# One operand format changed: the FFN's matmuls of a scan-and-FFN kernel take fp32 operands instead of two fp16 parts of each

## The chip, the cores and the metric

The kernel runs on 1 core of one Trainium2 chip. The metric is the device time of one execution in microseconds (us). Before the change it was 1563.5 us, the median of 3 runs (1563.49 to 1563.74).

## What is computed

The reference, cut to what matters (B = 8 rows, T = 256 time steps, N = 512 neurons, I = 1408 hidden units):

```python
# L0_cond: 256 steps of RK4 over q, p [8, 512]; drive is x, coupling [512, 512]
i_couple = tanh(q) @ coupling.T
dq = q - q**3 / 3 - p + drive + i_couple + bias      # four times in each step
dp = EPSILON * (q + ALPHA - BETA * p)
q, p = clip(rk4(q, p))                               # every q is kept: [8, 256, 512]
# L0_ffn on the 2048 rows of the q that were kept
w_gu = dequant_fp4(gate_up_packed, gate_up_scales)   # [2816, 512]
w_down = dequant_fp4(down_packed, down_scales)       # [512, 1408]
gate, up = split(q_trace @ w_gu.T)
y = (silu(gate) * up) @ w_down.T
out = x + y / sqrt(mean(y * y) + 1e-6)
```

The scan is serial: each of its 256 x 4 evaluations needs the one before. The FFN of a row needs only that row.

## The kernel before, in words

**Setup.** The weights arrive packed, in 11 units (`UNITS`). A unit holds, for 128 hidden features, the four 128-column tiles of the gate weights, the four of the up weights and the 512 columns of the down weights: 1536 columns (`UW`). For each unit SyncE issues two DMAs (`raw`, `sc`; three buffers, so that unit u + 3 is issued when `dq_w32` says that unit u is unpacked), VectorE runs three instructions (L547, L550, and L555, which writes fp32 `w32`), ScalarE rounds `w32` to the fp16 high part `wffn[:, u, 0]` (L513), and GpSimd forms the fp16 low part `wffn[:, u, 1]` by a subtraction (L501). Between units 3 and 4 VectorE also makes the scan's weights (L566). All engines meet at the end of the setup before the scan begins.

**Scan.** The program is 16 blocks (`BLOCKS`) of 16 time steps; a block has 64 stages (4 evaluations a step). In a stage TensorE multiplies `tanh(q)` (fp16 high and low part, `th`) by `wscan` in 32 small matmuls (L607), VectorE reduces the result into the next `q` in two halves (L722, L724), ScalarE takes the next tanh (L643, L645), and TensorE begins the next stage. While TensorE works, VectorE forms the low part of tanh (L683) and the terms of q alone (L677 to L695).

**FFN.** It lies one block behind the scan. After its 32 scan matmuls, and before those of the next stage, TensorE issues in program order the FFN matmuls that a table (`plan.pe`) gives to this stage. `hist` keeps the q of a block (128 tokens). In stages 0 to 2 of the next block ScalarE and VectorE turn it into two fp16 parts, `xh` (L393) and `xl` (L398). Each gate or up weight tile then takes four fp16 matmuls of 128 columns (high and low weight by `xh` and `xl`, L346): 32 for each unit. ScalarE applies silu (L370), VectorE multiplies (`h32`, L377), ScalarE and VectorE split `h32` into `hh` and `hl` (L384, L389), and eight fp16 matmuls of 256 columns (L360) add the unit to `y_ps`. A unit's down matmuls come at least `DOWN_LAG` = 7 stages after its gate and up matmuls. At the end of an FFN block the sum of squares, its root and the output rows follow.

`ffn_schedule` charges a gate or up matmul 1 and a down matmul 2 and gives every stage the same budget of 8; the last unit's eight down matmuls come late and fall into stage 6 of the block after. `Places` hands out the stages in which VectorE gets `h32` and `hl`. The first FFN block has a table of its own (`FIRST_SCHEDULE`), which starts at stage 6 with 13 or 14 matmuls a stage.

Of the kernel before, what the change touches and what calls it, by code (L numbers as in the profile page):

```python
# [120 lines left out]
GU_PARTS = 4  # L121
DOWN_PARTS = 4
DOWN_LAG = 7
START_LATE = 4
CATCH_UP = 6


def ffn_schedule(late, catch_up):


    gate_ups = [(u, j) for u in range(UNITS) for j in range(2 * GU_PARTS * KT)]
    downs = [(u, j) for u in range(UNITS) for j in range(2 * DOWN_PARTS)]
    down_cost = N // 2 // P
    even = (len(gate_ups) + down_cost * (len(downs) - 2 * DOWN_PARTS)) / STAGES
    at, done, budget, s = {}, {}, 0.0, FFN_FIRST
    while gate_ups or downs:
        if s >= FFN_FIRST + late + catch_up:
            budget += even
        elif s >= FFN_FIRST + late:
            budget += even * (late + catch_up) / catch_up  # L140
        while gate_ups or downs:
            down_now = downs and s >= done.get(downs[0][0], s) + DOWN_LAG
            if not (down_now or gate_ups) or budget < (down_cost if down_now else 1):
                break
            u, j = (downs if down_now else gate_ups).pop(0)
            at.setdefault(s, []).append(("down" if down_now else "gate_up", u, j))
            budget -= down_cost if down_now else 1
            if not down_now and j == 2 * GU_PARTS * KT - 1:
                done[u] = s
        s += 1  # L150
    return at, done


class Places:


    def __init__(self):
        self.taken = {1, 2}

    def next(self, s):  # L160
        while s % 4 not in (1, 2) or s % STAGES in self.taken:
            s += 1
        self.taken.add(s % STAGES)
        return s


class Schedule:


    def __init__(self, late, catch_up):  # L170
        self.pe, gate_up = ffn_schedule(late, catch_up)
        places = Places()
        self.silu = {s + 1: u for u, s in gate_up.items()}
        self.h32, self.hh, self.hl = {}, {}, {}
        for u, s in gate_up.items():
            at = places.next(s + 2)
            self.h32[at] = self.hh[at] = u
            self.hl[places.next(at + 1)] = u
# [7 lines left out]
    def rest(self):  # L186

        return [{s: x for s, x in part.items() if s >= STAGES} for part in
                (self.pe, self.silu, self.h32, self.hh, self.hl)] + [self.norm_sum]


SCHEDULE = Schedule(0, 0)
FIRST_SCHEDULE = Schedule(START_LATE, CATCH_UP)
assert FIRST_SCHEDULE.rest() == SCHEDULE.rest()
# [3 lines left out]
class Signals:  # L198


    def __init__(self, new, tag, parity):
# [19 lines left out]
        self.xh_ready = sem("xh_ready")  # L221
        self.xl_ready = sem("xl_ready")
# [3 lines left out]
        self.hh_ready = sem("hh_ready")  # L226
        self.hl_ready = sem("hl_ready")
# [10 lines left out]
def program(nc, x, drive, cond_t, coupling_t, bias_t, packed, scales, out):  # L238
# [8 lines left out]
    with ctx:  # L247
# [4 lines left out]
        hist = sb("hist", [P, KT, STEPS, B])  # L252
# [18 lines left out]
        wffn = sb("wffn", [P, UNITS, 2, UW], F16)  # L271
# [49 lines left out]
        dq_hi = sem("dq_hi")  # L321
        dq_lo = sem("dq_lo")
# [12 lines left out]
        def gate_up(pe, f, g, u, j):  # L335

            b = (u + f.parity) % 2
            half, r = divmod(j, GU_PARTS * KT)
            kt, which = divmod(r, GU_PARTS)
            part, tokens = ((0, xh), (0, xl), (1, xh), (1, xl))[which]  # L340
            col = (half * KT + kt) * P
# [6 lines left out]
            if j == 2 * GU_PARTS * KT - 1:  # L348
                i.then_inc(f.gu_ready, 1)

        def down(pe, f, u, j):

            b = (u + f.parity) % 2
            if j == 0:
                pe.wait_ge(f.hl_ready, u + 1)
            which, half = divmod(j, 2)
            part, h = ((0, hh), (0, hl), (1, hh), (1, hl))[which]
            cols = slice(half * N // 2, (half + 1) * N // 2)

            i = nc.tensor.matmul(y_ps[f.parity][:, cols], h[b][:, :], wffn[:, u, part, 2 * KT * P:][:, cols],  # L360
                                 start=(u == 0 and j == 0), stop=(u == UNITS - 1 and which == DOWN_PARTS - 1),
                                 skip_group_check=True)
            if j == 2 * DOWN_PARTS - 1:
                i.then_inc(f.down_done, 1)

        def ffn_silu(act, f, g, u):
# [4 lines left out]
                                 scale=1.0 / W_SCALE).then_inc(f.silu_ready, 1)  # L371

        def ffn_h32(dve, f, g, u):
            b = (u + f.parity) % 2
            dve.wait_ge(f.silu_ready, u + 1)
            wait_unit(dve, lambda s: s.hl_ready, f, g, u)
            nc.vector.scalar_tensor_tensor(h32[b][:, :], gu_ps[b][:, P:2 * P], H_SCALE / W_SCALE,  # L377
                                           silu[b][:, :], ALU.mult, ALU.mult).then_inc(f.h32_ready, 1)

        def ffn_hh(act, f, g, u):  # L380
            b = (u + f.parity) % 2
            act.wait_ge(f.h32_ready, u + 1)
            wait_unit(act, lambda s: s.down_done, f, g, u)
            nc.scalar.activation(hh[b][:, :], h32[b][:, :], ACT.Copy).then_inc(f.hh_ready, 1)  # L384

        def ffn_hl(dve, f, u):
            b = (u + f.parity) % 2
            dve.wait_ge(f.hh_ready, u + 1)
            nc.vector.tensor_tensor(hl[b][:, :], h32[b][:, :], hh[b][:, :], ALU.subtract).then_inc(f.hl_ready, 1)  # L389

        def hist_high(act, f, c):

            nc.scalar.activation(xh[f.parity][:, c, :], hist[:, c].rearrange("p t b -> p (t b)"), ACT.Copy,  # L393
                                 scale=1.0 / S).then_inc(f.xh_ready, 1)
# [27 lines left out]
        def act_ffn(act, plan, f, g, s):  # L422
# [3 lines left out]
            if s in plan.hh:  # L426
                ffn_hh(act, f, g, plan.hh[s])
# [3 lines left out]
        def dve_ffn(dve, plan, f, g, s):  # L431
# [3 lines left out]
            if s in plan.hl:  # L435
                ffn_hl(dve, f, plan.hl[s])
# [35 lines left out]
        with nc.Block() as block:  # L472
# [23 lines left out]
            def _(pool):  # L496
                nc.gpsimd.iota(shift[:, :], [[0, 1]], base=P - 1, channel_multiplier=-1).then_inc(iota_done, 1)
                nc.gpsimd.memset(mhalf[:, :], -0.5)
                for u in range(UNITS):
                    pool.wait_ge(dq_hi, u + 1)  # L500
                    nc.gpsimd.tensor_tensor(wffn[:, u, 1, :], w32[u % UNPACK_BUFS][:, :], wffn[:, u, 0, :],  # L501
                                            ALU.subtract).then_inc(dq_lo, 1)

            @block.scalar
            def _(act):
# [5 lines left out]
                for u in range(UNITS):  # L511
                    act.wait_ge(dq_w32, u + 1)
                    nc.scalar.activation(wffn[:, u, 0, :], w32[u % UNPACK_BUFS][:, :], ACT.Copy).then_inc(dq_hi, 1)  # L513
                    if u == 1:
                        act.wait_ge(coup_in, 16)
                        for n, coef in enumerate(COEF):
                            nc.scalar.activation(wscan[:, n, 0], coup[:, :, :], ACT.Copy,
                                                 scale=coef * S).then_inc(coup_hi, 1)

            @block.vector  # L520
            def _(dve):
# [9 lines left out]
                nc.vector.tensor_scalar(hist[:, :, STEPS - 1, :], q_raw[:, :, :], S, None, ALU.mult)  # L531
# [8 lines left out]
                link(nc.vector.tensor_copy(q_raw[:, :, :], hist[:, :, STEPS - 1, :]))  # L540

                def unpack(u):
# [10 lines left out]
                    if u >= UNPACK_BUFS:  # L553
                        dve.wait_ge(dq_lo, u - UNPACK_BUFS + 1)
# [394 lines left out]
```

## Time and profile before

| | |
|---|---|
| median of 3 runs | 1563.5 us |
| the profiled execution, its time | 1563.14 us |
| its span | 1561.4 us |
| TensorE busy (matmul) | 1434.9 us, 92% |
| TensorE weight load busy | 1306.2 us, 84% |
| VectorE busy | 1486.6 us, 95% |
| ScalarE busy | 785.3 us, 50% |
| GpSimd busy | 48.4 us, 3% |

The span is the profiled execution from its first to its last instruction; 1.7 us lie around it. The durations of matmuls are latencies: consecutive ones overlap, so a stream's pace is read from the distance between starts, or from a merged piece divided by its count. "Idle before" is the time in which the engine stood still ahead of an instruction, and the name behind the arrow is what ended it.

### The profile page before, as it was taken

To read this page: it belongs to the slowest core of one execution; us is meant where nothing else is said; L and a number is where in the kernel's file an instruction comes from. 1 tells how busy PE (TensorE), PEld (TensorE's weight loads), DVE (VectorE), ACT (ScalarE), POOL (GpSimd) and SP (SyncE) were. 2 spreads that over 40 slices of the span, in tenths; PEclk is the share of its full clock that TensorE was granted. 3 is DMA by queue.
4 is the path that set the end of the run, shared out by engine and by line. 5 is a ranking of instruction groups with operands and counts; after the bars stand their busy time and mean duration, and the time that the engine had idled before them with its cause. 6 is when DMAs were issued, how large, how long until landed. Compare 5 with 4: busy or idle time off the path is not lost.

```text
span 1561.4 us, 96622 instructions
## 1 busy us (share of the span) xinstructions
PE 1434.9 (92%) x39808; PEld 1306.2 (84%) x39808; DVE 1486.6 (95%) x11021; ACT 785.3 (50%) x5087; POOL 48.4 (3%) x49
## 2 busy tenths in 40 slices
PE   0047799999999999999999999999999999999997
PEld 0046799999999899999999999999989999999997
DVE  7989999999999999999999999999999999999992
ACT  4134455555555555555555555555555555555552
POOL 3410000000000000000000000000000000000000
PEclk9999999999999999999999999999999999999999
DMA  9500000000000000000000000000000000000000
GB/s 236 131 6 7 14 8 7 5 21 8 21 8 21 8 4 22 7 21 7 21 8 11 18 5 21 8 21 8 21 8 4 21 8 21 8 21 7 10 15 22
DMA packets 13548, 33.08 MB, mean 21 GB/s; under 512 B 1712, under 2 KB 6064, under 8 KB 12976
## 3 DMA queue, kind: packets, MB, share of 16 engines
q1 hardware_dynamic: 13104, 26.89, 6.6%
q8 instruction: 311, 5.10, 1.4%
q14 instruction: 133, 1.09, 0.2%
HBM read 22.69 MB, written 4.19 MB: 17 GB/s over the span
## 4 chain that ended last, share of the span: by engine, by line
DVE 82%; PE 10%; issue 2%; ACT 0%; DVEq 0%; POOLq 0%; POOL 0%; ACTq 0%
DVE th L683 12%; DVE with_q L677 9%; DVE scan_ps L695 8%; DVE q_cub L690 7%; DVE q_sq L687 7%; DVE q_stage L724 7%; DVE p_part L677 6%; DVE q_stage L722 6%; PE scan_ps L607 5%; PE gu_ps L346 4%; DVE with_p L677 3%; DVE q_raw L724 3%; DVE hist L706 3%; DVE h L377 3%; DVE q_raw L722 2%; DVE hl L389 2%
## 5 line engine op out<-in xcount | busy, mean ns | idle before, releaser
L607 PE MATMUL scan_ps<-th,wscan 128*128 128x32 f16 (+1 forms) x32768 | 1045.0, 175 | 118.0 <-ACT th L643 115.6
L607 PEld LDWEIGHTS scan_ps<-th,wscan 128*128 128x128 f16 x32768 | 939.2, 96 | 235.6 <-ACT th L643 179.6
L643 ACT ACTIVATE th<-q_stage 128x16 f16<-128x16 f32 x1536 | 318.4, 207 | 493.6 <-DVE q_stage L722 493.6
L346 PE MATMUL gu_ps<-xl,wffn 128*128 128x128 f16 x2816 | 385.2, 219 | 0.0
L346 PE MATMUL gu_ps<-xh,wffn 128*128 128x128 f16 x2816 | 384.7, 218 | 0.0
L683 DVE TENSOR_TENSOR th<-t,th 128x16 f16<-128x16 f32 x2048 | 351.5, 172 | 5.4 <-ACT t L645 5.4
L645 ACT ACTIVATE t<-q_stage 128x16 f32<-128x16 f32 x1536 | 306.1, 199 | 0.0
L346 PEld LDWEIGHTS gu_ps<-xl,wffn 128*128 128x128 f16 x2816 | 273.0, 97 | 0.3
L346 PEld LDWEIGHTS gu_ps<-xh,wffn 128*128 128x128 f16 x2816 | 262.9, 97 | 0.3
L643 ACT ACTIVATE th<-q_raw 128x16 f16<-128x16 f32 x512 | 106.2, 207 | 188.3 <-DVE q_raw L722 184.8
L452 ACT ACTIVATE sum_r<-dr,constant 128x64 f32<-128x64 f32 x528 | 174.1, 332 | 8.0 <-DMA dr<-drive 8.0
L724 DVE TENSOR_REDUCE q_stage<-scan_ps 128x16 f32<-128x48 f32 x768 | 159.7, 208 | 0.3
L722 DVE TENSOR_REDUCE q_stage<-scan_ps 128x16 f32<-128x48 f32 x768 | 157.5, 205 | 1.2 <-PE scan_ps L607 1.2
L695 DVE SCALAR_TENSOR_TENSOR scan_ps<-with_q,q_cub 128x32 f32<-128x32 f32 x768 | 152.2, 198 | 0.0
L687 DVE SCALAR_TENSOR_TENSOR q_sq<-q_stage 128x32 f32<-128x32 f32 x768 | 143.8, 187 | 3.4
L690 DVE SCALAR_TENSOR_TENSOR q_cub<-q_sq,q_stage 128x32 f32<-128x32 f32 x768 | 144.9, 189 | 0.0
L677 DVE SCALAR_TENSOR_TENSOR p_part<-p_part,q_stage 128x32 f32<-128x32 f32 x768 | 143.4, 187 | 0.0
L677 DVE SCALAR_TENSOR_TENSOR with_q<-hist,with_p 128x32 f32<-128x32 f32 x768 | 141.6, 184 | 0.0
L677 DVE SCALAR_TENSOR_TENSOR with_q<-q_stage,with_q 128x32 f32<-128x32 f32 x768 | 141.3, 184 | 0.0
L360 PE MATMUL y_ps<-wffn,hh 128*128 128x256 f16 x704 | 133.7, 271 | 2.3 <-DVE hl L389 2.3
L360 PE MATMUL y_ps<-wffn,hl 128*128 128x256 f16 x704 | 134.1, 272 | 0.0
L645 ACT ACTIVATE t<-q_raw 128x16 f32<-128x16 f32 x512 | 102.0, 199 | 0.0
(43 smaller groups left out, 990.8 us busy)
## 6 DMA issues: line engine op xcount, KB each, us to landing
raw<-packed SPq DMA_DIRECT2D x11, 768.0 KB, 6.2
dr<-drive SPq DMA_DIRECT2D x34, 128.0 KB, 3.3
sc<-scales SPq DMA_DIRECT2D x11, 384.0 KB, 6.3
xres<-x SPq DMA_DIRECT2D x16, 256.0 KB, 3.6
out<-osb SPq DMA_DIRECT2D x16, 256.0 KB, 2.9
coup<-coupling_t SPq DMA_DIRECT2D x1, 1024.0 KB, 15.7
q_raw<-cond_t SPq DMA_DIRECT2D x1, 16.0 KB, 1.8
bias<-bias_t SPq DMA_DIRECT2D x1, 2.0 KB, 1.7
```

What stands on the lines that cost most here:

```text
L346: i = nc.tensor.matmul(gu_ps[b][:, half * P:(half + 1) * P], wffn[:, u, part, col:col + P], tokens[f.parity][:, kt, :], start=(r == 0), st ...
L360: i = nc.tensor.matmul(y_ps[f.parity][:, cols], h[b][:, :], wffn[:, u, part, 2 * KT * P:][:, cols], start=(u == 0 and j == 0), stop=(u == ...
L607: i = nc.tensor.matmul(to if both else to[:, 0], wscan[:, w, part, kt, cols], moving if both else moving[:, 0], start=first, stop=last, sk ...
L643: nc.scalar.activation(th[s % 2][:, c, 0, :], q[:, c, :], ACT.Tanh, scale=1.0 / S).then_inc(now.tanh_hi, 1)
L645: nc.scalar.activation(t32[:, c, :], q[:, c, :], ACT.Tanh, scale=1.0 / S).then_inc(now.tanh_32, 1)
L677: return local(nc.vector.scalar_tensor_tensor(to, x, factor, base, ALU.mult, ALU.add))
L683: nc.vector.tensor_tensor(th[s % 2][:, c, 1, :], t32[:, c, :], th[s % 2][:, c, 0, :], ALU.subtract).then_inc(now.tanh_lo, 1)
L687: return local(nc.vector.scalar_tensor_tensor(q_sq[:, :, :], q, CUBE[i], q, ALU.mult, ALU.mult))
L690: return local(nc.vector.scalar_tensor_tensor(q_cub[:, :, :], q_sq[:, :, :], OWN[i], q, ALU.add, ALU.mult))
L695: nc.vector.scalar_tensor_tensor(local_ps, halves(linear[i]), UNIT[i], halves(q_cub[:, :, :]), ALU.mult, ALU.add).then_inc(now.first_half, 1)
L722: nc.vector.tensor_reduce(q_next[:, 0:HC, :], three[0], AX.X, ALU.add).then_inc(now.q_ready, 1)
L724: nc.vector.tensor_reduce(q_next[:, HC:KT, :], three[1], AX.X, ALU.add).then_inc(now.q_ready, 1)
```

## The change

`xh`, `xl`, `hh`, `hl`, `w32` and all that makes them are gone. VectorE's third unpacking instruction writes `wffn` in fp32 directly. The gate and up matmuls read `hist` in fp32 (now two buffers, one for each parity of blocks, since TensorE reads it during the whole block), and the down matmuls read `h32` in fp32. So a gate or up weight tile takes one matmul instruction where it took four, and a unit's down weights take two of 256 columns where they took eight. In one FFN block there are 88 gate and up matmuls and 22 down matmuls. They are dealt out by their number alone: gate and up number n goes to stage 2 + n * 64 // 88, down number n to a first stage + n * 64 // 22. The first FFN block uses the same table. `Places` now lets VectorE's `h32` fall into every stage that is not the fourth of its step.

```diff
-GU_PARTS = 4
-DOWN_PARTS = 4
-DOWN_LAG = 7
-START_LATE = 4
-CATCH_UP = 6
...
+DOWN_PARTS = 2
...
-    def __init__(self, late, catch_up):
-        self.pe, gate_up = ffn_schedule(late, catch_up)
+    def __init__(self):
+        gate_ups = [(u, j) for u in range(UNITS) for j in range(2 * KT)]
+        downs = [(u, j) for u in range(UNITS) for j in range(DOWN_PARTS)]
+        gate_up_at = [FFN_FIRST + n * STAGES // len(gate_ups) for n in range(len(gate_ups))]
+        done = [gate_up_at[(u + 1) * 2 * KT - 1] for u in range(UNITS)]
...
+        down_first = max(s - DOWN_PARTS * u * STAGES // len(downs) for u, s in enumerate(ready))
+        self.pe = {}
+        for n, (u, j) in enumerate(downs):
+            self.pe.setdefault(down_first + n * STAGES // len(downs), []).append(("down", u, j))
+        for n, (u, j) in enumerate(gate_ups):
+            self.pe.setdefault(gate_up_at[n], []).append(("gate_up", u, j))
...
-        hist = sb("hist", [P, KT, STEPS, B])
+        hist = [sb(f"hist{i}", [P, KT, STEPS, B]) for i in range(2)]
...
-        wffn = sb("wffn", [P, UNITS, 2, UW], F16)
+        wffn = sb("wffn", [P, UNITS, UW])
...
-            if u == 0 and half == 0 and which == 0:
-                pe.wait_ge(f.xl_ready, kt + 1)
-            i = nc.tensor.matmul(gu_ps[b][:, half * P:(half + 1) * P], wffn[:, u, part, col:col + P],
-                                 tokens[f.parity][:, kt, :], start=(r == 0), stop=(r == GU_PARTS * KT - 1))
...
+            i = nc.tensor.matmul(gu_ps[b][:, half * P:(half + 1) * P], wffn[:, u, j * P:(j + 1) * P],
+                                 hist[1 - f.parity][:, kt].rearrange("p t b -> p (t b)"),
+                                 start=(kt == 0), stop=(kt == KT - 1))
...
-                pe.wait_ge(f.hl_ready, u + 1)
...
+                pe.wait_ge(f.h32_ready, u + 1)
+            cols = slice(j * N // DOWN_PARTS, (j + 1) * N // DOWN_PARTS)
+            i = nc.tensor.matmul(y_ps[f.parity][:, cols], h32[b][:, :], wffn[:, u, 2 * KT * P:][:, cols],
+                                 start=(u == 0 and j == 0), stop=(u == UNITS - 1), skip_group_check=True)
...
-        def ffn_hh(act, f, g, u):
...
-        def ffn_hl(dve, f, u):
...
-        def hist_high(act, f, c):
...
-        def hist_low(dve, f, c):
...
-                for u in range(UNITS):
-                    pool.wait_ge(dq_hi, u + 1)
-                    nc.gpsimd.tensor_tensor(wffn[:, u, 1, :], w32[u % UNPACK_BUFS][:, :], wffn[:, u, 0, :],
-                                            ALU.subtract).then_inc(dq_lo, 1)
...
-                for u in range(UNITS):
-                    act.wait_ge(dq_w32, u + 1)
-                    nc.scalar.activation(wffn[:, u, 0, :], w32[u % UNPACK_BUFS][:, :], ACT.Copy).then_inc(dq_hi, 1)
...
-                    if u >= UNPACK_BUFS:
-                        dve.wait_ge(dq_lo, u - UNPACK_BUFS + 1)
-                    nc.vector.scalar_tensor_tensor(w32[b][:, :], fp4, FP4_BITS * W_SCALE, sc[b][:, :],
+                    nc.vector.scalar_tensor_tensor(wffn[:, u, :], fp4, FP4_BITS, sc[b][:, :],
                                                    ALU.mult, ALU.mult).then_inc(dq_w32, 1)
...
-                if ffn and t == 1:
-                    dve.wait_ge(now.xl_ready, KT)
+                ffn_part(s)
+                if t == 1 and rest:
+                    dve.wait_ge(before.gu_ready, UNITS)
```

**TensorE, in the steady part of a block.** Before, a stage with four down matmuls is followed by the 32 scan matmuls (12 with one tanh part, 20 with two) and by a stage with eight gate matmuls:

```order
L360 MATMUL y_ps<-wffn,hh 128x256 x2
L360 MATMUL y_ps<-wffn,hl 128x256 x2
L607 MATMUL scan_ps<-th,wscan 128x2x8 x12
L607 MATMUL scan_ps<-th,wscan 128x2x2x8 x20
L346 MATMUL gu_ps<-xh,wffn 128x128
L346 MATMUL gu_ps<-xl,wffn 128x128
L346 MATMUL gu_ps<-xh,wffn 128x128
L346 MATMUL gu_ps<-xl,wffn 128x128
L346 MATMUL gu_ps<-xh,wffn 128x128
L346 MATMUL gu_ps<-xl,wffn 128x128
L346 MATMUL gu_ps<-xh,wffn 128x128
L346 MATMUL gu_ps<-xl,wffn 128x128
```

Now, in a steady block too, a stage with one down and one gate matmul, then one with two gate matmuls, then one with one:

```order
L318 MATMUL y_ps<-wffn,h_1 128x256
L306 MATMUL gu_ps<-hist,wffn 128x128
L529 MATMUL scan_ps<-th,wscan 128x2x8 x12
L529 MATMUL scan_ps<-th,wscan 128x2x2x8 x20
L306 MATMUL gu_ps<-hist,wffn 128x128 x2
L529 MATMUL scan_ps<-th,wscan 128x2x8 x12
L529 MATMUL scan_ps<-th,wscan 128x2x2x8 x20
L306 MATMUL gu_ps<-hist,wffn 128x128
L529 MATMUL scan_ps<-th,wscan 128x2x8 x12
L529 MATMUL scan_ps<-th,wscan 128x2x2x8 x20
```

Four fp16 matmuls have become one fp32 matmul, and a stage now has one, two or three of them. Counted in fp16 matmuls of 128 columns (a down matmul of 256 columns is two), every stage had 8; if an fp32 matmul stands for four, a stage now has 4, 8, 12 or 16. Over the 64 stages of a block whose table overlaps the end of the one before, 24 stages have one gate matmul, 18 have two, 16 have one gate and one down, and 6 have two gates and one down.

**TensorE, stage 6 of a block.** Before, the last unit's eight down matmuls of the block before meet eight gate matmuls:

```order
L360 MATMUL y_ps<-wffn,hh 128x256 x2
L360 MATMUL y_ps<-wffn,hl 128x256 x2
L360 MATMUL y_ps<-wffn,hh 128x256 x2
L360 MATMUL y_ps<-wffn,hl 128x256 x2
L346 MATMUL gu_ps<-xh,wffn 128x128
L346 MATMUL gu_ps<-xl,wffn 128x128
L346 MATMUL gu_ps<-xh,wffn 128x128
L346 MATMUL gu_ps<-xl,wffn 128x128
L346 MATMUL gu_ps<-xh,wffn 128x128
L346 MATMUL gu_ps<-xl,wffn 128x128
L346 MATMUL gu_ps<-xh,wffn 128x128
L346 MATMUL gu_ps<-xl,wffn 128x128
```

This pile of 24 (in the same count) is gone: the last unit's two down matmuls fall into stages 5 and 8, one in each, with one gate matmul beside each.

**ScalarE, the setup.** Before, eleven roundings of whole units stand between the drive sums and the scan:

```order
L452 ACTIVATE sum_r<-dr,constant 128x8x8 x16
L513 ACTIVATE wffn<-w_0 128x1536
L513 ACTIVATE wffn<-w_1 128x1536
L517 ACTIVATE wscan<-coup 128x2048 x3
L513 ACTIVATE wffn<-w_2 128x1536
L513 ACTIVATE wffn<-w_0 128x1536
```

Now:

```order
L384 ACTIVATE sum_r<-dr,constant 128x8x8 x16
L441 ACTIVATE wscan<-coup 128x2048 x3
L404 UNCONDITIONAL_BRANCH
L800 UNCONDITIONAL_BRANCH
L567 ACTIVATE th<-q_raw 128x2x8
```

The roundings are gone, and with them GpSimd's eleven subtractions; VectorE's three instructions a unit stand in the same order as before.

## Rows read from the trace of the kernel before

**Rows 1.** The page, its first line.

```profile
span 1561.4 us, 96622 instructions
```

**Rows 2.** Busy time by stretch; (x) is instructions, then PEclk, DMA share, GB/s.

```profile
25.00:30.00 5.00, 0.00 (x0) 0.00 (x0) 4.93 (x4) 4.64 (x3) 1.51 (x2) 1.00 1.02 246
...
90.00:120.00 30.00, 21.26 (x649) 19.17 (x650) 27.28 (x207) 13.58 (x94) 1.42 (x1) 1.00 0.03 8
...
800.00:900.00 100.00, 99.88 (x2787) 90.60 (x2784) 98.23 (x771) 53.40 (x357) 0.74 (x2) 1.00 0.05 14
```

**Rows 3.** Timeline of VectorE: first reductions of chosen stages.

```profile
181.73 0.21 DVE L722 TENSOR_REDUCE q_stage<-scan_ps 128x16 f32<-128x48 f32 x1
...
197.74 0.21 DVE L722 TENSOR_REDUCE q_stage<-scan_ps 128x16 f32<-128x48 f32 x1
...
199.27 0.21 DVE L722 TENSOR_REDUCE q_raw<-scan_ps 128x16 f32<-128x48 f32 x1
...
272.61 0.21 DVE L722 TENSOR_REDUCE q_stage<-scan_ps 128x16 f32<-128x48 f32 x1
...
817.48 0.20 DVE L722 TENSOR_REDUCE q_stage<-scan_ps 128x16 f32<-128x48 f32 x1
...
819.58 0.21 DVE L722 TENSOR_REDUCE q_raw<-scan_ps 128x16 f32<-128x48 f32 x1 [0.69 <-PE scan_ps L607]
...
830.55 0.21 DVE L722 TENSOR_REDUCE q_raw<-scan_ps 128x16 f32<-128x48 f32 x1
...
1433.66 0.21 DVE L722 TENSOR_REDUCE q_stage<-scan_ps 128x16 f32<-128x48 f32 x1
```

**Rows 4.** The chain in order of time, the last 40 us: start, us, what.

```profile
1522.05 0.32 ACT xh L393
...
1522.40 0.90 DVE xl L398 x4
...
1525.27 4.47 PE gu_ps L346 x80
...
1529.73 0.87 PE y_ps L360 x8
...
1553.45 0.32 ACT hh L384
...
1553.79 0.30 DVE hl L389
```

**Rows 5.** Timeline of the setup: start, us, engine, line.

```profile
44.04 1.01 DVE L547 TENSOR_SCALAR nib<-raw,shift 128x1536 int32<-128x1536 int32 x1
...
47.76 1.01 DVE L547 TENSOR_SCALAR nib<-raw,shift 128x1536 int32<-128x1536 int32 x1
...
54.24 1.01 DVE L547 TENSOR_SCALAR nib<-raw,shift 128x1536 int32<-128x1536 int32 x1
...
88.33 3.09 POOL L501 TENSOR_TENSOR wffn<-w,wffn 128x1536 f16<-128x1536 f32 x1 [3.21 <-ACT wffn L513]
...
91.75 0.21 ACT L643 ACTIVATE th<-q_raw 128x16 f16<-128x16 f32 x1 [3.49 <-PEq L472]
```

**Rows 6.** Groups of the setup on VectorE: xcount, busy us, mean ns.

```profile
L555 DVE SCALAR_TENSOR_TENSOR w<-nib,sc 128x1536 f32<-128x1536 f16 x11 | 41.6, 3778 | 0.4
...
L550 DVE TENSOR_SCALAR nib<-nib 128x1536 int32<-128x1536 int32 x11 | 13.3, 1211 | 0.4
...
L566 DVE SCALAR_TENSOR_TENSOR wscan<-coup,wscan 128x2048 f16<-128x2048 f32 x3 | 9.6, 3241 | 0.0
```

**Rows 7.** DMA issues of the setup: KB each, median us to landing.

```profile
sc<-scales SPq DMA_DIRECT2D x11, 384.0 KB, 6.3
```

**Rows 8.** Groups of FFN instructions on TensorE: busy us, mean ns.

```profile
L346 PEld LDWEIGHTS gu_ps<-xl,wffn 128*128 128x128 f16 x2816 | 273.0, 97 | 0.3
```

**Rows 9.** Timeline of TensorE in the first FFN block.

```profile
190.74 0.31 PE L346 MATMUL gu_ps<-xh,wffn 128*128 128x128 f16 x1
...
190.84 0.31 PE L346 MATMUL gu_ps<-xl,wffn 128*128 128x128 f16 x1
```

More of the change, by code:

```diff
@@ L120, with free @@
 FFN_FIRST = 2
-GU_PARTS = 4
-DOWN_PARTS = 4
-DOWN_LAG = 7
-START_LATE = 4
-CATCH_UP = 6
[L128 to L151, printed above, removed]
+DOWN_PARTS = 2
 class Places:
     def __init__(self):
-        self.taken = {1, 2}
+        self.taken = set()
     def next(self, s):
-        while s % 4 not in (1, 2) or s % STAGES in self.taken:
+        def free(s):
+            if s % 4 == 0 and not {(s + 1) % STAGES, (s + 2) % STAGES} <= self.taken:
+                return False
+            return s % 4 < 3 and s % STAGES not in self.taken
+        while not free(s):
             s += 1
@@ L167 @@
 class Schedule:
-    def __init__(self, late, catch_up):
-        self.pe, gate_up = ffn_schedule(late, catch_up)
+    def __init__(self):
[3 more added lines that the diff above has]
+        done = [gate_up_at[(u + 1) * 2 * KT - 1] for u in range(UNITS)]
         places = Places()
-        self.silu = {s + 1: u for u, s in gate_up.items()}
-        self.h32, self.hh, self.hl = {}, {}, {}
-        for u, s in gate_up.items():
+        self.silu = {s + 1: u for u, s in enumerate(done)}
+        self.h32, ready = {}, []
+        for u, s in enumerate(done):
             at = places.next(s + 2)
-            self.h32[at] = self.hh[at] = u
-            self.hl[places.next(at + 1)] = u
+            self.h32[at] = u
+            ready.append(at)
+        down_first = max(s - DOWN_PARTS * u * STAGES // len(downs) for u, s in enumerate(ready))
[4 more added lines that the diff above has]
+            self.pe.setdefault(gate_up_at[n], []).append(("gate_up", u, j))
         self.norm_sum = max(self.pe) + 1
@@ L184, in __init__ @@
         self.end = max(self.norm_out) + 1
[L186 to L194, printed above, removed]
+SCHEDULE = Schedule()
 assert UNITS % 2 == 1
@@ L320, in program @@
         dq_w32 = sem("dq_w32")
-        dq_hi = sem("dq_hi")
-        dq_lo = sem("dq_lo")
         stored = sem("stored")
@@ L354, in down @@
             if j == 0:
-                pe.wait_ge(f.hl_ready, u + 1)
[L356 to L363, printed above, removed]
+                pe.wait_ge(f.h32_ready, u + 1)
+            cols = slice(j * N // DOWN_PARTS, (j + 1) * N // DOWN_PARTS)
+            i = nc.tensor.matmul(y_ps[f.parity][:, cols], h32[b][:, :], wffn[:, u, 2 * KT * P:][:, cols],
+                                 start=(u == 0 and j == 0), stop=(u == UNITS - 1), skip_group_check=True)
+            if j == DOWN_PARTS - 1:
                 i.then_inc(f.down_done, 1)
@@ L579, in jobs @@
             if ffn:
-                here.append((SCHEDULE, now, before, s) if rest else (FIRST_SCHEDULE, now, None, s))
+                here.append((SCHEDULE, now, before if rest else None, s))
             return here
@@ L629, in pe_block @@
                 couple(s, 0, 1, 1).then_inc(now.second_half, 1)
+                if ffn and s == FFN_FIRST:
+                    pe.wait_ge(before.clipped, STEPS)
                 for job in jobs(now, before, ffn, rest, s):
@@ L646, in act_block @@
                                          scale=1.0 / S).then_inc(now.tanh_32, 1)
-                if ffn and s in (0, 1):
-                    if s == 0:
-                        act.wait_ge(before.clipped, STEPS)
-                    for c in range(s * HC, (s + 1) * HC):
-                        hist_high(act, now, c)
                 if s == 1 and before:
@@ L711, in ffn_part @@
                     dve_ffn(dve, *job)
-                if ffn and s in (1, 2):
-                    for c in range((s - 1) * HC, s * HC):
-                        hist_low(dve, now, c)
             def finish(s):
@@ L726, in dve_block @@
             for t in range(STEPS):
-                q1 = hist[:, :, (t - 1) % STEPS, :]
+                q1 = hist[now.parity][:, :, t - 1, :] if t else hist[1 - now.parity][:, :, STEPS - 1, :]
                 q2, q3, q4 = (x[:, :, :] for x in q_stage)
@@ L840, in pe_tail @@
                 pe_ffn(pe, SCHEDULE, before, now, s)
+            pe.wait_ge(before.clipped, STEPS)
             for s in range(SCHEDULE.end):
@@ L844, in act_tail @@
         def act_tail(act, now, before):
-            act.wait_ge(before.clipped, STEPS)
-            for c in range(KT):
-                hist_high(act, now, c)
             for s in range(STAGES, SCHEDULE.end):
@@ L854, in dve_tail @@
             dve.wait_ge(before.q_ready, 2 * STAGES)
-            nc.vector.tensor_scalar(hist[:, :, STEPS - 1, :], q_raw[:, :, :], -CLAMP * S, CLAMP * S,
+            nc.vector.tensor_scalar(hist[before.parity][:, :, STEPS - 1, :], q_raw[:, :, :], -CLAMP * S, CLAMP * S,
                                     ALU.max, ALU.min).then_inc(before.clipped, 1)
-            for c in range(KT):
-                hist_low(dve, now, c)
             for s in range(STAGES, SCHEDULE.end):
```

56 lines of the change are left out of this document (12 added, 44 removed).

## The prediction

> **What bounds the kernel now.** The first line of the page gives the span of 1561.4 us [rows 1]; the profiled execution took 1563.1 us, 0.4 below the median of 1563.5. The busy time by stretch comes next. While the scan runs without the FFN, TensorE is busy for 21.3 of 30 us; with the FFN it is busy for 99.9 of 100 us and VectorE for 98.2 [rows 2]. Both look full, so the busy shares don't decide; the distance between the first reductions of two stages does [rows 3]. From 819.58 to 830.55 lie eight stages with eight FFN matmuls' worth each: 1.371 us a stage. That is the serial loop (TensorE, reduction, tanh, TensorE), and the FFN is hidden in the hole that it leaves on TensorE.
>
> How large is the hole? Where a stage has more than it holds, TensorE sets the distance. In the tail TensorE has nothing else: 80 gate matmuls take 4.47 us, 0.056 each, and eight down matmuls 0.87 us, 0.109 each [rows 4]. Stage 6 of a block, with eight of each, took 819.58 - 817.48 = 2.10 us [rows 3]; less 8 x 0.056 + 8 x 0.109 = 1.32 that leaves 0.78 for the scan's matmuls. A stage of 13 gate matmuls in the first FFN block took 1.53 us (197.74 to 199.27) [rows 3], which leaves 0.80. I take 0.80. So a stage lasts the larger of 1.371 and 0.80 + its FFN work, and up to 0.57 us of that work is free. Before, every ordinary stage has 8 x 0.056 = 0.45: it fits.
>
> A whole block takes (1433.66 - 272.61) / 13 = 89.31 us; the first FFN block takes 272.61 - 181.73 = 90.88 [rows 3]. Ideal would be 64 x 1.371 = 87.7; the rest is stage 6 with its pile (0.73 too long) and the splitting of `hist` in stages 0 to 2.
>
> **Setup: what is removed.** VectorE needs 3.72 us for a unit while GpSimd is idle (44.04 to 47.76) and 6.48 while it subtracts (47.76 to 54.24) [rows 5]. The means say the same: 3.78 us for L555, 1.21 for L550 [rows 6]. Without the subtraction the 2.76 us a unit go, in nine units, and once in the scan's weights (9.6 us for three, of which some 2.8 [rows 6]). The scan's first tanh came at 91.75, behind GpSimd's last subtraction, which began at 88.33 and took 3.09 [rows 5]; that tail of ScalarE and GpSimd behind VectorE's last unit goes as well. What is late next are the loads. A unit's scales take 6.3 us from issue to landing [rows 7], some 7 for the pair of DMAs; it is 1.18 MB (384 KB of scales, twice that of packed words), and with the DMA engines full they move 246 GB/s [rows 2], 4.8 us for a unit. Walk through it: four units, the coupling matrix and the drive are 6.0 MB, in by 28 us; unit 3 is unpacked at 32; scan weights 9.6 - 2.8 = 6.8 until 39; units 4 to 6 at 3.7 each until 50. Unit 7 is issued when unit 4 is done, at 43, and lands at 50; units 8, 9 and 10 come 4.7 apart, the last at 64, unpacked at 67.5; first tanh 67.8. **Gain 91.75 - 67.8 = 24.0 us.** By VectorE alone it would be about 9 us more, and by slower loads 4 less.
>
> **FFN work in the scan: what is moved.** No row shows an fp32 matmul. From below, one pass of 0.056 for a gate matmul is excluded by no row; from above, four passes with each weight load fully exposed (0.097, the mean of a load [rows 8]) make 4 x (0.056 + 0.097) = 0.61. I take four passes at the pace of the four fp16 matmuls that it replaces, 0.224 for a gate and 0.436 for a down matmul, because the nearest rows, streams of the same tiles, show loads hidden behind the matmul ahead: a load lasts 0.097 and yet the pace is 0.056 [rows 4, 8]. A stage's first fp32 load stands behind 16- and 32-column matmuls, which hide little; I charge 0.05, half of one load, once a stage (both ends, 0 and 0.097, stay for the range).
>
> The new table gives 24 stages one gate (0.80 + 0.27 = 1.07, hidden), 18 two gates (1.30, hidden), 16 a gate and a down (0.80 + 0.05 + 0.66 = 1.51, 0.139 too long) and 6 two gates and a down (1.73, 0.363 too long). A stage with 4 gives nothing back, since the loop's 1.371 stands. So a block takes 87.74 + 16 x 0.139 + 6 x 0.363 = 92.15. The pile and the splitting stages of before are in the 89.31 that this replaces. 14 blocks x (92.15 - 89.31) = 39.8; the first FFN block, with 14 and 5 such stages, comes to 91.5, 0.6 more. **Loss 40.4 us.**
>
> "Weight-path perf modes" in "TensorE: Matmul & The Clock Gate" of the Trainium skill speaks against my choice: the fast weight load is not used for fp32 operands, and "LDWEIGHTS (loading the stationary operand)" there gives 128 / 1.2 = 107 ns for a slow one, an estimate by that page that no row here shows. With each of four passes waiting for such a load a gate matmul would cost 0.428, and the sum would be 1771 instead of 1578.
>
> **At no cost.** On VectorE `hl` and the splitting go; they were hidden behind TensorE in ordinary stages, so nothing comes back beyond the above. The new waits (TensorE for the last clip at stage 2, VectorE for `gu_ready` at stage 4, the `h32` instruction for `down_done`) are for work at least a stage old; if one were late it would hold the clip and with it the loop, some tenths of a us a block. `hist` in two buffers adds no instruction.
>
> **Tail.** 11 x (8 x 0.224 + 2 x 0.436) = 29.3 us, as before. What goes is the splitting of `hist`, 0.32 + 0.90, and the last `hh` and `hl`, 0.32 + 0.30 [rows 4]: 1.8 us.
>
> **Sum.** 1563.1 - 24.0 + 40.4 - 1.8 = 1577.7, so **1578 us**, 0.9% slower. With the first load free it is 1561, with all of it exposed 1593.
>
> **Rivals.**
> *Fewer passes (faster).* If the two parts of an operand go through together and an fp32 matmul costs two fp16 ones, 0.112 and 0.218, the fullest stage is 0.80 + 0.44 = 1.24: all hidden. Blocks of 87.7 give -25.1, the tail loses 14.6 more: 1498 us. For it: one instruction stands where four stood. Against: no row shows a pass doing more than one fp16 part. It decides once a gate, a down and the exposed load together cost under 0.67 us instead of my 0.71: there the loss in the scan equals the gains.
> *One load exposed in each fp32 matmul.* Gate 0.321, down 0.533; a stage with both takes 1.65, with two gates 1.44: blocks of 97.2, scan +115.3, tail +10.7: 1663 us. For it: fp32 weights are twice the bytes of an fp16 tile. Against: the hiding seen in [rows 4, 8].
> *Loads set the pace of every pass.* At 0.097 a pass a gate costs 0.388 and a down still 0.436: blocks of 101.3, scan +177.7, tail +14.4: 1729 us, and beyond 2000 with all four exposed on top.
> *The clock.* In the first FFN block matmuls stand 0.10 to 0.11 apart (190.74, 190.84) [rows 9] though the same tiles later take 0.056: TensorE's lower level of 1.2 GHz against 2.4, after a block with the scan alone, while the granted clock column reads 1.00 [rows 2]. If stages with a single gate matmul let it fall back for good, gate and down double: blocks of some 119, about 2010 us. Against: the mean work of a stage, 8.25 fp16 matmuls' worth, is that of before, and full stages raise it again. The page named above says that the chip's clock is held down after idle time and released by work; that points to before's even stages as the safer ones, with the same 2010.
> *The change does nothing*, because setup and scan cancel, is the low end of my own forecast (1561).
>
> **How the numbers follow.** My case has 0.66 (1561 to 1593, a few us lower if the loads keep up with VectorE); one exposed load 0.13; loads setting the pace 0.09; fewer passes 0.08; the clock 0.04. The range 1555 to 1665 holds the first two, 0.79. This kernel's measurement tells changes over 0.2%, 3.1 us, from none. Slower: 0.26 of the last kinds and 0.49 of my case, 0.75. Within 0.2% (1560.4 to 1566.6): 0.12. Faster: 0.08 and 0.05 from my case's low end, 0.13.
>
> **What would show it.** First tanh near 68 us, GpSimd idle in the setup, the third unpacking instruction at some 1.8 us in every unit (3.72 less two of about 1.0), VectorE waiting for `sc` from unit 7 on. Stages of 1.37 with one or two gates, 1.51 with a gate and a down, 1.73 with the third. A tail stream of 0.22 a gate and 0.44 a down. If two-gate stages take over 1.40, an fp32 matmul costs more than I say; if stages with a down take 1.37 too, it has fewer passes than four.

## The result

The changed kernel takes 1588.2 us (median, 1587.22 to 1588.61) against 1563.49 on the same chip: 1.0158 times the time of before, 95% interval [1.014, 1.0175]. The forecast was 1578, in a range of 1555 to 1665. Its profiled execution has a span of 1586.8 us where [rows 1] has 1561.4, 25.4 more.

The page's first line and the chain that ended last, by engine and by line:

```profile
span 1586.8 us, 88883 instructions
...
PE 84%; DVE 9%; issue 1%; ACT 1%; POOL 0%; POOLq 0%; DVEq 0%; ACTq 0%
...
PE scan_ps L529 51%; PE gu_ps L306 22%; PE y_ps L318 12%; DVE th L601 1%; DVE with_q L595 1%; DVE q_stage L637 1%; DVE q_sq L605 1%; DVE scan_ps L613 1%; DVE q_stage L639 1%; DVE q_cub L608 1%; DVE q_raw L639 1%; DVE q_raw L637 1%; DVE hist L624 1%; ACT th L567 0%; DVE p_part L595 0%
```

The line by engine on the page of the kernel before:

```profile
DVE 82%; PE 10%; issue 2%; ACT 0%; DVEq 0%; POOLq 0%; POOL 0%; ACTq 0%
```

84% of the chain now lies on TensorE, where 82% of it lay on VectorE: before, VectorE's instructions followed one another almost without a gap and TensorE was in time; here TensorE is late in so many stages that the chain runs through it.

The first reductions (L637 here, L722 before) of chosen stages, beside [rows 3]:

```profile
248.37 0.21 DVE L637 TENSOR_REDUCE q_stage<-scan_ps 128x16 f32<-128x48 f32 x1 [0.29 <-PE scan_ps L529]
...
529.33 0.21 DVE L637 TENSOR_REDUCE q_stage<-scan_ps 128x16 f32<-128x48 f32 x1
...
531.10 0.21 DVE L637 TENSOR_REDUCE q_raw<-scan_ps 128x16 f32<-128x48 f32 x1 [0.34 <-PE scan_ps L529]
...
533.86 0.21 DVE L637 TENSOR_REDUCE q_stage<-scan_ps 128x16 f32<-128x48 f32 x1
...
535.40 0.21 DVE L637 TENSOR_REDUCE q_stage<-scan_ps 128x16 f32<-128x48 f32 x1
...
536.79 0.21 DVE L637 TENSOR_REDUCE q_raw<-scan_ps 128x16 f32<-128x48 f32 x1
...
1455.39 0.21 DVE L637 TENSOR_REDUCE q_stage<-scan_ps 128x16 f32<-128x48 f32 x1 [0.29 <-PE scan_ps L529]
```

529.33 to 531.10 is a stage with two gates and a down: 1.77 us. 533.86 to 535.40 has a gate and a down: 1.54. 535.40 to 536.79 has one gate: 1.39, about what the loop takes alone. Thirteen blocks take 1455.39 - 248.37 = 1207.02 us, 92.85 each, against 89.31. Sorted by the table, the stages of the blocks from the third on, each the distance of two such rows, have these means: one gate 1.378 us (336 stages), two gates 1.380 (252), a gate and a down 1.533 (224), two gates and a down 1.746 (83).

The groups of the fp32 matmuls, and those of VectorE in the setup, beside [rows 6] and [rows 8]:

```profile
L306 PE MATMUL gu_ps<-hist,wffn 128*128 128x128 f32 x2816 | 526.1, 294 | 0.0
...
L306 PEld LDWEIGHTS gu_ps<-hist,wffn 128*128 128x128 f32 x2816 | 417.6, 191 | 17.7
...
L318 PE MATMUL y_ps<-wffn,h 128*128 128x256 f32 x704 | 236.8, 418 | 0.7 <-DVE h L334 0.5
...
L477 DVE SCALAR_TENSOR_TENSOR wffn<-nib,sc 128x1536 f32<-128x1536 f16 x11 | 19.3, 1759 | 0.4
...
L474 DVE TENSOR_SCALAR nib<-nib 128x1536 int32<-128x1536 int32 x11 | 10.6, 960 | 0.4
...
L488 DVE SCALAR_TENSOR_TENSOR wscan<-coup,wscan 128x2048 f16<-128x2048 f32 x3 | 6.7, 2285 | 0.0
```

One fp32 matmul instruction leaves two matmul records and two weight loads: 88 gates in 16 blocks are 1408, the group has 2816. A load's record has 191 ns here and 97 ns in fp16 [rows 8]. The means are latencies; the pace is in the tail's chain below. L477 and L474 are down from means of 3778 and 1211 ns to 1759 and 960. The three scan weights (L488) take 2285 ns each, 6.7 us in all. GpSimd has no work on the weights left.

The setup's timeline (start, us, engine, line), beside [rows 5]:

```profile
40.05 1.01 DVE L471 TENSOR_SCALAR nib<-raw,shift 128x1536 int32<-128x1536 int32 x1
...
43.76 1.01 DVE L471 TENSOR_SCALAR nib<-raw,shift 128x1536 int32<-128x1536 int32 x1
...
56.59 1.02 DVE L471 TENSOR_SCALAR nib<-raw,shift 128x1536 int32<-128x1536 int32 x1 [0.86 <-DMA sc<-scales]
...
65.10 0.22 ACT L567 ACTIVATE th<-q_raw 128x16 f16<-128x16 f32 x1 [38.43 <-PEq L404]
```

A unit takes 3.71 us (40.05 to 43.76); from unit 8 on VectorE waits for the loads (0.86 us before 56.59); the first tanh comes at 65.10 instead of 91.75.

The chain in order of time, in the tail, beside [rows 4]:

```profile
1553.39 0.21 DVE h L334
...
1553.64 0.70 PE y_ps L318 x2
...
1575.32 0.89 PE gu_ps L306 x8
...
1576.21 0.43 PE y_ps L318 x2
```

Eight records are four gates, in 0.89 us: 0.222 for one, and a down of 256 columns takes 0.43. Four fp16 matmuls took 0.224 and 0.436.

**Where the time went.** Between the first reduction of the scan and the last one lie 1428.55 us before (92.88 to 1521.43) and 1480.98 after (66.24 to 1547.22): +52.4. Ahead of it 26.6 are saved, behind it 0.4. Together that makes 25.4, the difference of the spans.

### The profile page after: what moved, and what is told of

Read it like the earlier page. It is cut to its first block, busy times and chain, and to the rows that moved or that the text cites. A ratio compares the mean times of both kernels' runs of the same rounds, so it can differ in the third digit from the quotient of the medians.

```text
span 1586.8 us, 88883 instructions
## 1 busy us (share of the span) xinstructions
PE 1478.8 (93%) x36288; PEld 1378.2 (87%) x36288; DVE 1460.7 (92%) x10781; ACT 717.6 (45%) x4836; POOL 12.2 (1%) x38
## 4 chain that ended last, share of the span: by engine, by line
PE 84%; DVE 9%; issue 1%; ACT 1%; POOL 0%; POOLq 0%; DVEq 0%; ACTq 0%
PE scan_ps L529 51%; PE gu_ps L306 22%; PE y_ps L318 12%; DVE th L601 1%; DVE with_q L595 1%; DVE q_stage L637 1%; DVE q_sq L605 1%; DVE scan_ps L613 1%; DVE q_stage L639 1%; DVE q_cub L608 1%; DVE q_raw L639 1%; DVE q_raw L637 1%; DVE hist L624 1%; ACT th L567 0%; DVE p_part L595 0%
## 5 line engine op out<-in xcount | busy, mean ns | idle before, releaser
L529 PE MATMUL scan_ps<-th,wscan 128*128 128x32 f16 (+1 forms) x32768 | 1018.8, 175 | 101.2 <-ACT th L567 87.7
L529 PEld LDWEIGHTS scan_ps<-th,wscan 128*128 128x128 f16 x32768 | 950.5, 96 | 182.6 <-ACT th L567 174.9
L306 PE MATMUL gu_ps<-hist,wffn 128*128 128x128 f32 x2816 | 526.1, 294 | 0.0
L306 PEld LDWEIGHTS gu_ps<-hist,wffn 128*128 128x128 f32 x2816 | 417.6, 191 | 17.7
L318 PE MATMUL y_ps<-wffn,h 128*128 128x256 f32 x704 | 236.8, 418 | 0.7 <-DVE h L334 0.5
L637 DVE TENSOR_REDUCE q_stage<-scan_ps 128x16 f32<-128x48 f32 x768 | 158.8, 207 | 37.9 <-PE scan_ps L529 18.7
L318 PEld LDWEIGHTS y_ps<-wffn,h 128*128 128x128 f32 x704 | 105.4, 189 | 1.8 <-DVE h L334 1.6
L595 DVE SCALAR_TENSOR_TENSOR with_p<-p_state,sum_r 128x128 f32<-128x128 f32 x256 | 74.7, 292 | 0.0
L334 DVE SCALAR_TENSOR_TENSOR h<-gu_ps,silu 128x128 f32<-128x128 f32 x176 | 49.6, 282 | 24.8 <-ACT silu L327 24.3
```

The costliest lines, as they stand in the source:

```text
L318: i = nc.tensor.matmul(y_ps[f.parity][:, cols], h32[b][:, :], wffn[:, u, 2 * KT * P:][:, cols], start=(u == 0 and j == 0), stop=(u == UNIT ...
L529: i = nc.tensor.matmul(to if both else to[:, 0], wscan[:, w, part, kt, cols], moving if both else moving[:, 0], start=first, stop=last, sk ...
L595: return local(nc.vector.scalar_tensor_tensor(to, x, factor, base, ALU.mult, ALU.add))
L637: nc.vector.tensor_reduce(q_next[:, 0:HC, :], three[0], AX.X, ALU.add).then_inc(now.q_ready, 1)
```

## The experiments

The question is twofold: whether the scan lost to the format or to the way in which the matmuls are dealt out, and whether the setup gained because GpSimd is silent. All edits are made to the changed kernel, but for the fourth.

### GpSimd's subtractions put back

```diff
+                nc.gpsimd.memset(dead_in[:, :], 0.0).then_inc(dead_set, 1)
+                pool.wait_ge(dead_set, 1)
+                for u in range(UNITS):
+                    pool.wait_ge(dq_w32, u + 1)
+                    nc.gpsimd.tensor_tensor(dead_out[:, u, :], wffn[:, u, :], dead_in[:, :], ALU.subtract)
```

> The changed kernel with GpSimd's eleven subtractions put back in the setup, on a tile that nobody reads, started as soon as VectorE has unpacked a unit. If VectorE's instructions are slowed by GpSimd working beside them, they go back from 3.7 to about 6.5 us a unit, the first tanh comes at 86 to 91 us instead of 65.1, and the kernel takes 1609 to 1614 us. The rival, that VectorE had waited for the rounding and subtraction chain through its buffers, leaves the unpacking as it is: first tanh at about 68.5 us (the last subtraction alone is behind it), 1591 to 1592 us.

It took 1611.5 us. Timeline of its setup:

```profile
45.99 3.79 POOL L438 TENSOR_TENSOR dead_out<-wffn,dead_in 128x1536 f16<-128x1536 f32 x1 [10.35 <-DVE wffn L485]
...
46.88 3.73 DVE L482 TENSOR_SCALAR nib<-nib 128x1536 int32<-128x1536 int32 x1
...
84.89 3.09 POOL L438 TENSOR_TENSOR dead_out<-wffn,dead_in 128x1536 f16<-128x1536 f32 x1 [2.69 <-DVE wffn L485]
...
88.29 0.22 ACT L575 ACTIVATE th<-q_raw 128x16 f16<-128x16 f32 x1 [61.46 <-PEq L407]
```

The second unpacking instruction (960 ns alone) started at 46.88 while GpSimd was at work from 45.99 to 49.78, and lasted 3.73 us, until 50.61: it stood still until GpSimd was done and ended 0.83 after it. Nothing reads GpSimd's output and VectorE waits for no signal of it, so the rival falls. The kernel before shows the same delay in another instruction: L555 took 4.52 us beside GpSimd (from 49.80) and 1.76 without it (from 46.08), 2.76 more. The first tanh comes at 88.29 instead of 65.10, 23.2 us later, which is what the whole kernel lost (1611.5 - 1588.2 = 23.3). Some 20 of them are VectorE's: its last multiplication ends at 84.82 here and at 64.81 in the changed kernel. The other 3.2 are the last subtraction, from 84.89 to 87.98: the setup and the scan are two blocks of the program (`with nc.Block()`), and the second began 0.3 us behind the last engine of the first in both kernels, whether or not something read its output. "SBUF: two separate sides" in "SBUF — State Buffer" of the Trainium skill says that the two engines take a shared pair of memory ports by an exclusive lock, for a whole instruction, and that the loser fully blocks. By that rule the second unpacking instruction ends about one length of its own after GpSimd's, and the trace agrees: 0.83 us after 49.78, where it takes 0.96 alone.

### Another table, evenly filled

```diff
-        gate_up_at = [FFN_FIRST + n * STAGES // len(gate_ups) for n in range(len(gate_ups))]
...
+            slots = [s for s in range(FFN_FIRST, FFN_FIRST + STAGES) if s % STAGES not in alone]
+            more = len(gate_ups) - 2 * len(slots)
+            third = {[s for s in slots if s % 4 == 2][(2 * k + 1) * 11 // (2 * more)] for k in range(more)}
+            gate_up_at = [s for s in slots for _ in range(3 if s in third else 2)]
```

`alone` are the 22 stages that have a down matmul. The first stage with a down and the places of `h32` follow from it.

> The changed kernel with another table: a stage has two gate matmuls or one down matmul, four stages of a block have three gate matmuls. Nothing else moves. If the loss in the scan comes from stages whose FFN work is over the 0.57 us that a stage leaves free, 60 stages take 1.38 us and four take 1.54: a block of 88.9 us instead of 92.85, and 1588 less 15 x 3.95, 1528 to 1532 us, below both kernels. The rival, that every stage with fp32 matmuls is a little longer whatever the table, leaves the block near 92.8 and the time at 1585 to 1590 us.

It took 1524.5 us, 0.9755 times the kernel before, [0.9738, 0.9771]: faster than both. Its first reductions:

```profile
423.14 0.21 DVE L646 TENSOR_REDUCE q_stage<-scan_ps 128x16 f32<-128x48 f32 x1
...
511.54 0.21 DVE L646 TENSOR_REDUCE q_stage<-scan_ps 128x16 f32<-128x48 f32 x1
...
525.16 0.21 DVE L646 TENSOR_REDUCE q_stage<-scan_ps 128x16 f32<-128x48 f32 x1
...
526.72 0.21 DVE L646 TENSOR_REDUCE q_raw<-scan_ps 128x16 f32<-128x48 f32 x1
...
528.09 0.21 DVE L646 TENSOR_REDUCE q_stage<-scan_ps 128x16 f32<-128x48 f32 x1
```

This block takes 88.40 us (423.14 to 511.54; the mean of 13 is 88.48), less than the 89.31 of before. A stage with three gates takes 1.56 (525.16 to 526.72), the next with two 1.37. Stages with two gates have a mean of 1.368, with one down 1.378, with three gates 1.552. The scan alone, in the first block of the program, takes 1.389 a stage. So fp32 matmuls do not lengthen a stage whose work fits, and the rival falls.

### A needless fp16 matmul ahead of the fp32 ones

```diff
+                here = jobs(now, before, ffn, rest, s)
+                if any(plan.pe.get(at) for plan, _, _, at in here):
+                    nc.tensor.matmul(cover_ps[:, 0:P], wscan[:, 0, 0, 0, 0:P], wscan[:, 0, 0, 1, 0:P],
+                                     start=True, stop=True)
```

> The changed kernel with one needless fp16 matmul of 128 columns ahead of the FFN work of each stage, into a bank of its own; it takes 0.056 us. If the 0.07 us by which full stages exceed 0.80 plus the stream's pace is the first fp32 weight load, it runs behind the needless matmul: stages with a gate and a down stay at 1.53 to 1.55 us, and the kernel at 1588 to 1593 us. The rival, that the 0.07 is something that no matmul covers (a start-up of the fp32 stream, or slower scan matmuls behind it), adds 0.056 to each of the 22 full stages of a block: 1.59 and 1.80 us, 1605 to 1608 us.

It took 1597.4 us. Two of its first reductions, around the stage with a gate and a down that took 1.54 above:

```profile
535.73 0.21 DVE L642 TENSOR_REDUCE q_stage<-scan_ps 128x16 f32<-128x48 f32 x1
...
537.29 0.21 DVE L642 TENSOR_REDUCE q_stage<-scan_ps 128x16 f32<-128x48 f32 x1
```

The means went from 1.533 to 1.560 and from 1.746 to 1.773: 0.027 more where the added matmul is 0.056. Neither expectation fits. The timeline of TensorE shows where the time lies. In the changed kernel, the last scan matmul of such a stage and its two records of a down:

```profile
533.85 0.18 PE L529 MATMUL scan_ps<-th,wscan 128*128 128x32 f16 x1
533.87 0.46 PE L318 MATMUL y_ps<-wffn,h 128*128 128x256 f32 x1
...
534.17 0.38 PE L318 MATMUL y_ps<-wffn,h 128*128 128x256 f32 x1
```

With the needless matmul:

```profile
535.74 0.22 PE L557 MATMUL cover_ps<-wscan 128*128 128x128 f16 x1
535.79 0.43 PE L319 MATMUL y_ps<-wffn,h 128*128 128x256 f32 x1
...
536.06 0.38 PE L319 MATMUL y_ps<-wffn,h 128*128 128x256 f32 x1
```

The fp32 stream doesn't begin late: its first record starts 0.025 us behind the last scan matmul, as the first fp16 one does in the kernel before. The time is lost inside the first fp32 matmul of the stage. Its first record has 463 ns and the second comes 0.30 behind it, where a later down record has 379 and 0.215; for a gate it is 356 ns against 275. The weight loads say why. In a stream of gates a load starts together with the matmul ahead of its own, 0.11 before its own, and is covered. The first fp32 load of a stage starts at 533.85, together with the last scan matmul and 0.025 before its own matmul. The second starts at 533.96, 0.11 behind the first; so a load takes some 0.11, and 0.11 - 0.025 = 0.08 of the first stay uncovered, which is what the record is longer by. The needless matmul starts 0.055 before the first fp32 one, so it covers 0.03 more and not its whole 0.056, and the record falls from 463 to 433 ns. So the term is the first weight load, most of it exposed. The 0.11 is worked out from these distances; no run measures a load by itself.

### The fp16 kernel with the new dealing

The edit is made to the kernel before, for both tables:

```diff
+    for n, (u, j) in enumerate(gate_ups):
+        s = FFN_FIRST + n // 4 * 4 * STAGES // len(gate_ups)
+        at.setdefault(s, []).append(("gate_up", u, j))
+        done[u] = s
...
+        first = max(s - 2 * u * STAGES // (2 * UNITS) for s, u in self.hl.items())
...
+        for n, (u, j) in enumerate(downs):
+            self.pe.setdefault(first + n // 4 * STAGES // (2 * UNITS), []).append(("down", u, j))
```

> The kernel before, fp16 parts and all, with its matmuls dealt out as the changed kernel deals its own: groups of four fp16 matmuls where that has one fp32 matmul, gates by the same numbers, downs from stage 12 on. 14 stages of a block have a gate and a down group, 8 have two gates and a down. If the dealing alone makes the loss in the scan, the first take 0.80 + 0.66 = 1.46 us and the second 1.68, a block takes 91.3 to 91.8 us against 89.31, and the kernel 1590 to 1598 us. The rival, that the fp32 format makes it, leaves the block at 89 to 89.6 and the time at 1560 to 1567 us.

It took 1602.4 us, 1.0253 times the kernel before, [1.0236, 1.027]. Its first reductions:

```profile
562.24 0.21 DVE L715 TENSOR_REDUCE q_stage<-scan_ps 128x16 f32<-128x48 f32 x1
...
563.70 0.21 DVE L715 TENSOR_REDUCE q_stage<-scan_ps 128x16 f32<-128x48 f32 x1
...
566.46 0.21 DVE L715 TENSOR_REDUCE q_stage<-scan_ps 128x16 f32<-128x48 f32 x1
...
568.12 0.21 DVE L715 TENSOR_REDUCE q_stage<-scan_ps 128x16 f32<-128x48 f32 x1 [0.16 <-PE scan_ps L600]
```

1.46 us for a stage with a gate group and a down group (562.24 to 563.70; the mean of 196 is 1.460, as worked out), 1.66 with two gate groups and a down (mean 1.668). Its scan lasts 1467.4 us from first to last reduction (92.16 to 1559.54), 38.8 more than before, without one fp32 operand. So the dealing makes most of the loss of 52.4. The run also sizes the other term: a stage with a gate and a down takes 0.073 more in fp32 (1.533 against 1.460), one with two gates and a down 0.078 more (1.746 against 1.668). That is the first weight load, less 0.008 by which 0.222 + 0.43 are under 0.66. The time is 4 us above the expected range: a block takes 91.99 us (mean of 13) where 91.3 to 91.8 were expected. I had counted the stages that split `hist` low (1.54 and 1.60 in stages 0 and 1). The two kernels' blocks differ by these stages and by 8 longest stages here against 6 there, so 52.4 is not the sum of 38.8 and the fp32 term.

### Down matmuls of 64 columns

```diff
-DOWN_PARTS = 2
+DOWN_PARTS = 8
```

> The changed kernel with the down matmuls cut into 64 columns each (8 for a unit instead of 2), dealt out evenly: 24 stages with one gate and two downs, 24 with two gates and one down, 16 with one of each. If an fp32 matmul costs its passes over the columns, a down of 64 columns costs 0.109 us, the stages take 1.38 to 1.43 us, a block 89.3, and the kernel 1533 to 1540 us. The rival, that below some width the weight loads set its pace, at about 0.107 us for each of two loads, makes it 0.21: stages of 1.52 to 1.53 in 48 of 64, a block of 95.2 us, a tail 9 us longer, 1625 to 1640 us.

It took 1655.2 us. The chain in its tail:

```profile
1625.43 0.28 PE gu_ps L306 x2
...
1625.71 0.17 PE y_ps L318 x2
...
1625.88 0.50 PE gu_ps L306 x4
...
1626.38 0.39 PE y_ps L318 x4
...
1626.77 0.28 PE gu_ps L306 x2
```

From 1625.43 to 1626.77 lie three gates and three downs in 1.34 us; less 3 x 0.222, a down of 64 columns costs 0.225, as much as a gate of 128. A stage with a gate and two downs took 1.558, one with two gates and a down 1.552. The rival was right in kind: half the columns make the matmul no cheaper, and the loads in the stages of this run start 0.11 us apart, so at 64 columns the two weight loads set the pace. The time is 15 us over its range: I had charged 0.21 for a down and 1.52 to 1.53 for 48 stages, and a block takes 96.7 us instead of 95.2. In "TensorE: Matmul & The Clock Gate" of the Trainium skill, "LDWEIGHTS (loading the stationary operand)" gives the number of columns over 1.2 as a load's ns, which makes 107 for 128 columns, an estimate by that page. The trace agrees in the pace, 0.225 / 2 = 0.11; a load's record lasts 191 ns. The prediction had used the page's figure for a load in each of four passes; the trace has two load records for each matmul.

### Down matmuls of 512 columns

```diff
-DOWN_PARTS = 2
+DOWN_PARTS = 1
```

> The changed kernel with one down matmul of 512 columns for each unit, 11 a block. By the rule that a stage takes the larger of 1.38 and 0.87 plus its FFN work, with 0.87 for such a down and 0.22 for a gate, 8 stages of a block take 1.96 us, 3 take 2.19 and 53 take 1.38: a block of 95.4 us, 1588 + 15 x 2.6 = 1624 to 1630 us. The rival, that fewer and wider matmuls help because half of the weight loads of the down matmuls go, gives 1580 to 1588 us.

It took 1621.4 us. The stage with one gate and one such down:

```profile
541.28 0.21 DVE L637 TENSOR_REDUCE q_stage<-scan_ps 128x16 f32<-128x48 f32 x1
...
543.25 0.21 DVE L637 TENSOR_REDUCE q_stage<-scan_ps 128x16 f32<-128x48 f32 x1 [0.54 <-PE scan_ps L529]
```

1.97 us, mean 1.963 where the rule gives 1.96, and 2.173 where it gives 2.19; a block takes 94.9. The total is 3 us under the expected range. The rival falls: half the loads of the down matmuls bring nothing, and a coarser piece costs what it is over the hole.

## Why the prediction was right, step by step

- **The hole.** "A stage lasts the larger of 1.371 and 0.80 + its FFN work": shown. The fp16 kernel with the new dealing gave 1.460 for 0.80 + 0.66.
- **The path behind 1.371.** I named TensorE, reduction, tanh, TensorE. The chain before has 82% on VectorE and 0% on ScalarE, so VectorE's own instructions lay end to end on it. The figure was read as a distance and didn't suffer. Whether VectorE's work or the loop through the tanh sets it no run separates; the scan alone takes as long (1.389) with no FFN work on VectorE.
- **Price of an fp32 matmul.** 0.224 and 0.436 were forecast, 0.222 and 0.43 measured. The rivals of fewer passes, of an exposed load in every matmul and of loads setting every pass at 0.097 are out at these widths. My reason, loads hidden behind the matmul ahead, held by little: two loads of 0.11 make 0.22, as much as a gate lasts, and at half the width they decide. That it held for gates was in part luck.
- **The first load.** I charged 0.05 a stage, half of a load of 0.097, with 0 and 0.097 as the ends; measured are 0.073 to 0.078. This is the largest part of what I was short in the scan: 16 stages of a block were forecast at 1.51 and took 1.533, 6 at 1.734 and took 1.746, which over 14 blocks makes 6 us. The time lies in the first fp32 matmul of the stage, and its load was nearly all exposed, not half.
- **The hidden stages.** They took 1.378 to 1.380, not 1.371: 42 of them in 14 blocks make 5 us. Most stages take 1.34 to 1.41 as before and single ones up to 1.77; I had read the loop from eight stages without such a one. It isn't the fp32 format: before, ordinary stages with eight gate matmuls had a mean of 1.376, and the first block of the program, the scan alone, takes 88.9 us in both kernels, 1.389 a stage. So the "ideal" 87.7 of the prediction was too low. What delays single stages I didn't test.
- **The first FFN block.** 93.22 us against 91.5 forecast and 90.88 before. Its stages 2 to 4 took 1.89, 1.47 and 1.89: two gates and the step to the next scan matmul take 1.00 us there (157.91 to 158.91), and later 0.53.

```profile
157.91 1.20 PE L306 MATMUL gu_ps<-hist,wffn 128*128 128x128 f32 x4
158.91 1.06 PE L529 MATMUL scan_ps<-th,wscan 128*128 128x16 f16 x32
...
536.80 0.69 PE L306 MATMUL gu_ps<-hist,wffn 128*128 128x128 f32 x4
537.33 0.97 PE L529 MATMUL scan_ps<-th,wscan 128*128 128x16 f16 x32
```

By that pace, nearly twice as slow, TensorE was at the lower level of its clock, as in [rows 9]. It then stayed at the higher level, in even and uneven stages alike, so the clock rival is out. The granted clock column reads 1.00 throughout.
- **Loss in the scan.** +52.4 where 40.4 was forecast: the three terms above, 6 + 5 + 1.7, within 1 us.
- **Setup.** 26.6 saved where 24.0 was forecast. The walk had the order right, VectorE first and the loads from then on, but VectorE waits from unit 8 on and not from unit 7. Unit 3 was unpacked 2.4 us earlier than I had it, at 29.6: from 5 to 30 us the loads moved 252 to 324 GB/s and not 246.
- **Tail.** 0.4 saved where 1.8 was forecast. The splitting is gone, but `h32` now stands behind the output rows of the block before until 1553.39, and the down matmul starts at 1553.64. I had named the work that went away there and not what would be late next.
- **Sum.** 1563.1 - 26.6 + 52.4 - 0.4 = 1588.5. The direction and the mechanism stand. The loss in the scan was 12 us too small, and the setup, 2.6 too small a gain, hid some of that. The change in all was forecast at 15 us and measured at 25, in a range that reached up to 1665: the sign and the sum of its parts are borne out, the size only roughly.

The version that the experiments point to, fp32 operands with the even table, is 64 us under the changed kernel and 38 under the one before: 26.6 of these come from the setup and 10.6 from the scan (1417.99 us from first to last reduction, against 1428.55), where the stages of splitting and the pile are gone and four stages of three gates a block have come.

## What to carry to other kernels

When background work is dealt into the holes of a serial loop, an operand format that merges four instructions into one makes the pieces coarser: count the largest sum that one hole gets, not the mean. Here an fp32 matmul of 128 or 256 columns costs as much as the four fp16 ones that it replaces, and saves the engines that made the parts; at 64 columns it costs as much as at 128. The first one behind a stream of short fp16 matmuls costs 0.08 more. Before work is given to GpSimd beside VectorE, ask what VectorE runs then: here each subtraction of 3.3 us cost VectorE 2.8.

## What the runs showed that I had not expected

An fp32 matmul leaves two loads and two matmul records, not one or four. A down matmul of 64 columns costs the same 0.225 us as a matmul of 128 columns. And the first fp32 matmul behind the scan's fp16 matmuls takes 0.08 us longer than one in a stream: its weight load starts only 0.025 us ahead of it, and a needless fp16 matmul in front covers no more than 0.03.
